# The third low part of a MoE group's hidden layer moved from GpSimd to VectorE

## The reference, cut to what matters

```
x = x + MoE_A(groupnorm(x))        # 8 images of 32x32 tokens x 96; 8 experts, top 2, hidden 384
t = t + attention(layernorm(t))    # 6 heads of 16, causal over 1024 tokens
t = t + MoE_C(layernorm(t))        # 4 experts, top 2, hidden 384
# MoE:  h = gelu(x @ W1[e] + b1[e]) ;  y = h @ W2[e] + b2[e] ;  out = sum_e gate[e] * y
```

## Time and profile before

| | |
|---|---|
| median of 3 runs | 1542.0 us (1541.95 to 1543.82) |
| span of the profiled execution, first to last instruction | 1533.6 us |
| runs' median less that span | 8.4 us |
| TensorE busy | 1324.4 us, 86% |
| ScalarE busy | 934.1 us, 61% |
| VectorE busy | 893.8 us, 58% |
| GpSimd busy | 716.0 us, 47% |

### The profile page before, as it was taken

One profiled execution on the slowest core, in us unless ns is written; L12 is line 12 of the kernel. 1 busy time (PEld: TensorE's weight loads), 2 busy tenths in 40 slices (PEclk: granted clock), 3 DMA queues, 4 the chain that ended last, 5 costly groups with the idle time before them and its releaser, 6 DMA issues.

```text
span 1533.6 us, 36404 instructions
## 1 busy us (share of the span) xinstructions
PE 1324.4 (86%) x12957; PEld 775.0 (51%) x12957; DVE 893.8 (58%) x2662; ACT 934.1 (61%) x1880; POOL 716.0 (47%) x656
## 2 busy tenths in 40 slices
PE   4778879888898899889898899888998898968978
PEld 1554543565536564466635565365644665333445
DVE  4865593388617784287724886177832866165362
ACT  2566537566675667656675667656676666703755
POOL 4765540467406572367605573075713665000355
PEclk9897998999999999899998999899999999956989
DMA  5000200300021000400004000210003000120100
GB/s 108 12 1 18 46 1 12 75 2 2 12 54 32 2 2 23 71 7 2 2 22 76 1 2 16 52 32 2 2 23 65 1 2 2 38 48 1 23 12 11
DMA packets 37424, 35.14 MB, mean 23 GB/s; under 512 B 26091, under 2 KB 28012, under 8 KB 37234
## 3 DMA queue, kind: packets, MB, share of 16 engines
q1 hardware_dynamic: 20594, 26.37, 8.8%
q10 hardware_dynamic: 16640, 6.29, 1.9%
HBM read 22.62 MB, written 9.63 MB: 21 GB/s over the span
## 4 chain that ended last, share of the span: by engine, by line
PE 30%; issue 26%; POOL 21%; DVE 13%; DMA 4%; ACT 2%; DVEq 1%; POOLq 1%; SPq 1%; ACTq 0%
POOL hidl L628 20%; PE ps_y L647 11%; PE ps_u L647 9%; PE ps_r L647 6%; DVE mpart L1156 4%; PE ps_m L647 3%; DVE xn L1138 1%; DMA ks<-qk_dram 1%; DMA qk_dram<-qk_l 1%; DVE acc L1104 1%; ACT hidh L934 1%; DVE yt L1288 1%; POOLq L608 1%; PE ps_m L666 1%; POOL rstd L609 1%
## 5 line engine op out<-in xcount | busy, mean ns | idle before, releaser
L628 POOL TENSOR_TENSOR hidl<-hid,hidh 128x512 f16<-128x512 f32 x576 | 670.7, 1185 | 686.2 <-ACT hidh L934 684.1
L933 ACT ACTIVATE hid<-ps_u 128x512 f32<-128x512 f32 x576 | 345.0, 599 | 391.8 <-PE ps_u L647 363.2
L1156 DVE TENSOR_REDUCE mpart<-ps_r 128x1 f32<-128x512 f32 (+2 forms) x576 | 297.3, 549 | 94.1 <-PE ps_r L647 79.8
L934 ACT ACTIVATE hidh<-ps_u 128x512 f16<-128x512 f32 x576 | 344.4, 598 | 0.0
L647 PEld LDWEIGHTS ps_y<-w2s,hidh 128*128 128x128 f16 x4608 | 276.4, 101 | 119.2 <-issue 24.1
L647 PE MATMUL ps_y<-w2s,hidh 128*128 128x96 f16 x4608 | 326.3, 210 | 8.0 <-DVE acc L1104 7.2
L647 PE MATMUL ps_r<-ks,qs 96*128 96x512 f16 (+2 forms) x576 | 199.9, 363 | 66.9 <-DVE mpart L1156 39.4
L647 PE MATMUL ps_y<-w2s,hidl 128*128 128x96 f16 x2304 | 231.0, 211 | 26.7 <-POOL hidl L628 26.6
L647 PE MATMUL ps_u<-xah,w1h 97*128 97x512 f16 x408 | 168.7, 414 | 29.8 <-ACT hidh L934 12.8
L965 ACT ACTIVATE probs<-ps_r 128x512 f32<-128x512 f32 (+3 forms) x352 | 152.9, 506 | 57.6 <-PE ps_r L647 57.2
L647 PE MATMUL ps_u<-xah,w1l 97*128 97x512 f16 x408 | 168.1, 412 | 0.0
(11 more groups left out here) (188 smaller groups left out, 1582.0 us busy)
## 6 DMA issues: line engine op xcount, KB each, us to landing
rb<-rsum_dram SPq DMA_DIRECT2D x24, 256.0 KB, 4.2
qs<-qk_dram SPq DMA_DIRECT2D x24, 192.0 KB, 4.9
ks<-qk_dram SPq DMA_DIRECT2D x24, 192.0 KB, 4.8
xin<-in_x_dram ACTq DMA_DIRECT2D x8, 384.0 KB, 4.1
qk_dram<-qk_h SPq DMA_DIRECT2D x16, 192.0 KB, 3.1
qk_dram<-qk_l SPq DMA_DIRECT2D x16, 192.0 KB, 3.5
out_dram<-xo ACTq DMA_DIRECT2D x8, 384.0 KB, 3.0
w_raw<-in_L_conv_W_dram SPq DMA_DIRECT2D x8, 288.0 KB, 5.1
```

The lines of the kernel that those rows point to most:

```text
L628: g.tensor_tensor(hidl[:, grp.k % 2, j, :], hid[:, j, :], hidh[:, grp.k % 2, j, :], ALU.subtract).then_inc(hl_ready, 1)
L933: a.activation(hid[:, j, :], bank[:], ACT.Gelu, scale=1.0 / WS)
L934: a.activation(hidh[:, grp.k % 2, j, :], bank[:], ACT.Gelu, scale=1.0 / WS).then_inc(h_ready, 1)
L1156: v.tensor_reduce(mpart[:, h, i, part:part + 1], ps_r[k % 3][:, 0:w], AX, ALU.max).then_inc(mx_free, 1)
```

## The change

GpSimd forms `hidl` of chunks 0 and 1 only. VectorE forms chunk 2's in slot 3 of each group, before that slot's chores and before `combine`, and signals on a semaphore of its own, `hd_ready`. TensorE waits for both semaphores, ScalarE for the one of its chunk.

```diff
@@ GpSimd
-                        if up and j < HT:
+                        if up and j < HT - 1:
                             pool.wait_ge(h_ready, grp.value(HT, j + 1))
                             g.tensor_tensor(hidl[:, grp.k % 2, j, :], hid[:, j, :], hidh[:, grp.k % 2, j, :],
@@ TensorE, second_layer
-                    pe.wait_ge(hl_ready, grp.value(HT, 0))
+                    pe.wait_ge(hl_ready, grp.value(HT - 1, 0))
+                    pe.wait_ge(hd_ready, grp.value(1, 0))
@@ ScalarE
-                            wait(act, hl_ready, grp.value(HT, j + 1 - HT))
+                            if j < HT - 1:
+                                wait(act, hl_ready, grp.value(HT - 1, j + 1 - (HT - 1)))
+                            else:
+                                wait(act, hd_ready, grp.value(1, 0))
@@ VectorE, moes
                     for slot in slots:
+                        if up and slot % TC == TC - 1:
+                            ahead = 1 if down else 0
+                            j = HT - 1
+                            dve.wait_ge(h_ready, grp.value(HT, HT * ahead + HT))
+                            v.tensor_tensor(hidl[:, (grp.k + ahead) % 2, j, :], hid[:, j, :],
+                                            hidh[:, (grp.k + ahead) % 2, j, :], ALU.subtract).then_inc(hd_ready, 1)
                         run_chores(m, chore, chores(it, phase, slot))
```

More of the change, by code:

```diff
@@ L437, in build @@
         up_full, h_ready = sem("up_full"), sem("h_ready")
-        hl_ready = sem("hl_ready")
+        hl_ready, hd_ready = sem("hl_ready"), sem("hd_ready")
         y_full, y_free = sem("y_full"), sem("y_free")
```

## The result

The changed kernel takes 1552.4 us at the median (four runs, 1550.8 to 1562.5) beside 1542.0 for the kernel before in the same session: +10.4 us, ratio 1.0108, 95% interval 1.0063 to 1.0154. The forecast was 1539.6, -2.4 us. The time falls in the range, near what rival A gave, but the sign is the other one.

What follows compares the result with a forecast made beforehand. TensorE was taken as the bound, with GpSimd and VectorE having room on average. Losses of 23.5 us less gains of 25.9 gave -2.4: 1542.0 to 1539.6 us, range 1530 to 1553 (forecast's own 1535 to 1543).

Steps and rivals of the forecast that it cites:

- rival A: VectorE's queue and shared access decide: late subtracts at slots 7, 11, 15 each meet a GpSimd operation; 1550 us, chance 0.32.
- The price, 0.69 us: VectorE's new 128x512 subtract in slot 3 was taken at 0.69 us, bounded by 0.61 and 1.85.
- Over that stretch VectorE is idle 1.9 us a group, so this costs nothing.: Plain groups: slot-3 maximum and combine pushed back 0.7-0.9 us, absorbed by VectorE's average idle time at no cost.
- The gains, 25.9 us: Sum of savings, group by group where TensorE waited for hidl, including relief of VectorE operations: 25.9 us.
- Slots 24 to 27, -11.4: Group behind ln2's rstd: wait shrinks 0.5 and four xn operations end 1.4 earlier, in six images: 11.4 us saved.
- After `route_c`, -3.6: VectorE's small routing operations are held up by one GpSimd operation fewer: 0.6 us in six images, 3.6 saved.
- `sum_inverse`, +9.2: Slot 4's operation waits for a DMA; group 1's subtract behind it stops TensorE: 9.2 us lost over six images.
- MoE C, +5.7: Slots 8 to 19: subtracts behind ln1_apply and gn_apply; first stop even (-0.5), second +1.75: 5.7 us lost.
- The memset, +3.0: Slot 46's 5.18 us memset delays slot 47's subtract to 95.6, stopping TensorE: 3.0 us lost.
- Slots 60 to 63 and the last group, -6.2: TensorE's hidl waits shrink in slots 60 to 63 (3.0 us) and in the last group before the softmax (3.2).
- The base: Runs' median put 8.4 us above the profiled span of 1533.6, for launch and end around it.
- B: Relief decides, faster: xn relief and relief after route_c arrive, C stage even; 8 us more, 1531 us, chance 0.15.

Runs made afterwards that it cites:

- queue_only: relief_only plus a same-size VectorE subtract of still tiles each group, with no waits and nobody waiting for it: 1542.6 us, 1.0037 of the kernel before.
- relief_queue: relief_only plus VectorE's subtract of the real tiles into a spare tile, with VectorE's and ScalarE's waits but none by TensorE: 1.0051 of the kernel before.
- relief_only: The changed kernel with the third low part left out, a zeroed tile multiplied in its place: 1479.4 us, 0.9637 of the kernel before.
- pool_alone: relief_only plus a third GpSimd subtract of still tiles, after ScalarE's third chunk, its result awaited by nobody: 0.9989 of the kernel before.
- picked: The kernel before with VectorE forming the third low part in only three groups of an image, GpSimd in all others: 0.9900 of the kernel before.
- low_later: The kernel before with TensorE taking token tile 0's low products in slot 2, not slot 1; result invalid, only timed: 1534.1 us, 0.9989.
- picked_again: The same kernel as picked, timed a second time: 0.9931 of the kernel before.

## Why the prediction was wrong, step by step

- **The price, 0.69 us.** Right: 691 ns at the median, a mean of 746.
- **"Over that stretch VectorE is idle 1.9 us a group, so this costs nothing."** This is the step that failed. The average of idle time held for A12-15 (+2.2 us in all) and not for the groups with `ln2_apply`, routing, `ln1_apply` and `gn_apply`, nor for images 0 and 1. `queue_only` prices it at 61 us; the prediction's list of losses came to 23.5, all but a few of them TensorE's direct waits, which by `relief_queue` against the result are worth some 9.
- **The gains, 25.9 us.** Direction right, size wrong: `relief_only` shows 56. It named TensorE's waits for the third part; `pool_alone` shows that the operation costs about as much with nobody waiting for it. The two prices, 61 and 56, nearly cancel, and so did the prediction's two sums, each less than half of what was measured: that the forecast time fell within 1% is luck.
- **Slots 24 to 27, -11.4.** The worst term. Of it -3.0 was group 6's own wait. The wait shrank, but the mark stayed where it was against group 5's (+0.3 for -3.0): `rstd` starts 0.6 us later, as it waits for VectorE, which slot 23's subtract has put back (without that subtract, in `picked`, it starts as before, and the mark comes 3.6 us earlier). -8.4 was `xn`, and A6-7 came out at +3.2. Relief of the four `xn` was 0.9 us and not 1.4, and they start 1.2 us later against group 5's mark, with the subtracts of slots 23 and 27 ahead of them. The subtract was priced at its deadline for TensorE, never at the chore behind it.
- **After `route_c`, -3.6.** A8-11 came out at -2.9, within what two executions differ.
- **`sum_inverse`, +9.2.** Right: A0-5 falls by 10.1 when it moves. A0-5 as a whole was +13.3 for +6.2: groups 0 and 1 +12.0, of which two executions of the kernel before differ by 3.3, and group 6's own wait +0.3 for -3.0.
- **MoE C, +5.7.** Measured +7.3. The shape was wrong, though. The first stop did not come out even: group 2's mark came 8.6 us later over the six images for -3.0. At 933.53 TensorE waits 2.09 us, for a subtract that stood behind `ln1_apply` and took 1.50 us instead of 0.69, with GpSimd's low parts beside it, and the wait for a maximum comes on top. The second stop, behind `gn_apply`, did not come: group 3's mark -1.4 for some +8.7.

```profile
931.97 1.50 DVE L1122 TENSOR_TENSOR hidl<-hid,hidh 128x512 f16<-128x512 f32 x1
933.53 0.30 PE L647 MATMUL ps_y<-w2s,hidl 128*128 128x96 f16 x3 [2.09 <-DVE hidl L1122]
936.22 0.50 PE L647 MATMUL ps_r<-ks,qs 96*128 96x384 f16 x1 [1.19 <-DVE mpart L1167]
```

- **The memset, +3.0.** The stop is there, 5.74 us at 95.62. Images 0 and 1 together came to +3.7 for +2.1.
- **Slots 60 to 63 and the last group, -6.2.** Right: group 15's mark came 2.8 us earlier for 3.0, the last group's in six images 3.3 for 2.7. As much again, 3.4, fell in the softmax and the slots behind it and was not forecast. `picked` is built on these two and slots 24 to 27, and gains 11 to 15 us.
- **The base.** 8.4 us around the span was wrong by 6.7. A median and a profiled execution may be two different executions; where their distance is large, the profile is of an unusual one.
- **Rival A** had the right sign, and nearly the right time. Its queue was the cause; its mechanism, three late subtracts of an image each running into GpSimd, was so for one of the three, that of C slot 11 (1.50 us in all six images): of 192 subtracts 25 took over 0.8 us, 9 us above the median in all, and its sign (over 45 us of new waits, a mean above 1.0) did not show. B's relief of VectorE was real, and larger than B had it; the queue took it back. B's and C's times lie outside the interval.

## What to carry to other kernels

An operation has a price on an in-order engine wherever that engine is late, also when nobody waits for its result. Before moving one, walk the receiving engine's queue stretch by stretch and cost it at the chore behind it, not at its own deadline; busy shares of a stage hide this. A list of waits names the last releaser: removing 18 us of waits gave nothing (`low_later`), and an operation that stood in 27 us of them was worth 56. Where both engines are dear in the same stretches, choose groups, from the rows in which the wait is seen, and measure the choice.

## What the runs showed that was not expected

**Waits and the clock.** Span and mean granted clock of the kernel before and of `relief_only`:

```profile
core 0: 1533.6 us, clock 0.923
```

```profile
core 0: 1476.1 us, clock 0.936
```

The clock has two levels here, 2.4 GHz (1.00) and 1.2 GHz (0.50), so the lower one held for (1 - 0.923) x 2 x 1533.6 = 236 us before and 189 us with the relief; TensorE's busy time for the same instructions fell from 1324.4 to 1299.5. At most 25 of the 57.5 us between these two profiles are that. Busy time by stretch in the kernel before (length, PE, PEld, DVE, ACT, POOL, clock):

```profile
864.00:866.00 2.00, 2.00 (x28) 1.51 (x27) 1.30 (x5) 1.95 (x4) 1.16 (x1) 1.00 0.00 0
866.00:868.00 2.00, 0.61 (x15) 0.46 (x11) 1.16 (x4) 1.99 (x4) 0.00 (x0) 1.00 0.02 4
868.00:870.00 2.00, 1.47 (x10) 1.07 (x11) 0.61 (x3) 1.94 (x4) 1.63 (x2) 0.95 0.00 0
870.00:872.00 2.00, 2.00 (x11) 0.89 (x9) 1.85 (x13) 1.22 (x3) 1.28 (x2) 0.50 0.03 8
872.00:874.00 2.00, 2.00 (x21) 1.30 (x20) 1.17 (x11) 1.06 (x3) 1.52 (x2) 0.69 0.00 0
```

TensorE is busy 0.61 of 2 us after 866 and 1.47 of the next 2, and then its clock is at half: for 0.2 + 2.0 + 1.2 us of the last three stretches, by their 0.95, 0.50 and 0.69.

What the low clock costs depends on who is next. In the image shown in the earlier trace rows it held from about 853 to 856 us, and the wait for a maximum is 0.38 us and not 1.59:

```profile
855.92 0.49 PE L647 MATMUL ps_r<-ks,qs 96*128 96x512 f16 x1 [0.38 <-DVE mpart L1156]
```

TensorE's slower work filled the wait, and A6-7 took the same 13.45 us as in the three images like it: VectorE set the end. In `picked` it held from about 850 to 853, behind that wait, and A6-7 took 14.95 us where `picked_again` has 13.59; the next image shows the same. That is the 2.7 us between the two profiles of one kernel. In the 95 executions of the kernel before in the other four sessions, longer spans go with a lower clock (correlation -0.46 to -0.77 by session), so it goes with the spread of single runs; that it causes it was not tested.
